# Units of one image instead of a pair, with one GroupNorm chain for both norms and one order of operations for every step

## What is computed

```python
# _gn: GroupNorm over 32 groups of 6 channels and all tokens of an image
x = x + hadamard(_gn(x))                       # 192 -> 192 channels, a fixed matrix
h = _gn(x)
h = gelu(layernorm(h @ W1.T + b1) * g1 + beta1)   # layernorm over the channels of a token
h = gelu(layernorm(h @ W2.T + b2) * g2 + beta2)
x = x + (h @ W3.T + b3)
```

## Time and profile before

| | |
|---|---|
| runs | 929.77 and 929.75 us, median 929.76 |
| profiled execution, first to last instruction | 927.5 us |
| busy: PE, DVE, ACT, POOL | 831.8, 799.5, 814.3, 551.2 us |
| DMA | 81.99 MB, mean 88 GB/s |
| chain that ended last | PE 48%, DVE 31%, ACT 10%, POOL 7% |

### The profile page before, as it was taken

The page is one execution under the profiler, slowest core; times in us unless marked ns, Lnnn a source line. Parts: engine busy times, 40 slices in busy tenths (PEclk is TensorE's granted clock), DMA queues, the critical chain, the costliest instruction groups (busy, mean ns, idle before and its releaser), DMA issues.

```text
span 927.5 us, 22221 instructions
## 1 busy us (share of the span) xinstructions
PE 831.8 (90%) x8353; PEld 552.3 (60%) x8353; DVE 799.5 (86%) x1416; ACT 814.3 (88%) x2400; POOL 551.2 (59%) x414
## 2 busy tenths in 40 slices
PE   0646889899999999999999999999999999889897
PEld 0114545556666666666666666666666667566663
DVE  6699898999999999999999999999998887745455
ACT  0687879689999999999999999999999998999982
POOL 0452544566666666666666666766766666577760
PEclk9987999999999999999999999999999999999999
DMA  9725022223323333233233232332111113121213
GB/s 265 234 69 145 1 70 69 74 69 104 107 69 108 103 105 98 81 103 108 70 110 101 94 117 70 98 113 84 59 40 55 50 36 104 40 69 35 70 36 102
DMA packets 52090, 81.99 MB, mean 88 GB/s; under 512 B 14608, under 2 KB 14736, under 8 KB 51856
## 3 DMA queue, kind: packets, MB, share of 16 engines
q1 hardware_dynamic: 51984, 80.58, 28.8%
HBM read 41.23 MB, written 39.32 MB: 87 GB/s over the span
## 4 chain that ended last, share of the span: by engine, by line
PE 48%; DVE 31%; ACT 10%; POOL 7%; issue 2%; SPq 1%; DMA 1%; ACTq 0%; DVEq 0%; POOLq 0%
PE tm L578 11%; DVE z L1248 6%; PE tm L573 5%; PE tp L590 5%; DVE X L1089 5%; DVE xs_lo L1080 4%; POOL ge_lo L943 4%; PE hl L487 4%; DVE bn L1106 3%; DVE x_lo L1230 3%; PE hl L418 3%; ACT z L729 3%; PE tm L567 3%; PE hl L516 2%; PE hl L492 2%; PE hl L511 2%
## 5 line engine op out<-in xcount | busy, mean ns | idle before, releaser
L943 POOL TENSOR_TENSOR ge_lo<-ge,ge_hi 128x512 f16<-128x512 f32 (+1 forms) x190 | 314.1, 1664 | 189.7 <-ACT ge_hi L759 189.7
L729 ACT ACTIVATE z<-tm 128x194 f32<-128x194 f32 x784 | 250.8, 346 | 41.9 <-PE tm L578 38.6
L935 POOL TENSOR_TENSOR rs<-ssq,neg_half 128x4 f32<-128x4 f32 x196 | 204.9, 1046 | 124.1 <-ACT z L729 123.2
L1248 DVE TENSOR_TENSOR z<-tm,rs 128x768 f32<-128x768 f32 x196 | 186.0, 949 | 62.1 <-POOL rs L935 61.3
L729 ACT ACTIVATION_READ_ACCUMULATOR z<-tm 128x1 f32 x784 | 175.1, 223 | 0.0
L741 ACT ACTIVATE ge<-tp,par 128x512 f32<-128x512 f32 x196 | 155.2, 792 | 21.1 <-PE tp L590 20.5
L759 ACT ACTIVATE ge_hi<-ge 128x512 f16<-128x512 f32 (+1 forms) x190 | 161.8, 855 | 2.9
L1089 DVE SCALAR_TENSOR_TENSOR X<-hl,h_bias,X 128x512 f32<-128x512 f32 x138 | 102.0, 741 | 30.6 <-PE hl L423 30.1
L590 PE MATMUL tp<-cst,z 128*128 128x128 f32 x784 | 121.8, 278 | 4.9 <-DVE z L1248 2.8
L1230 DVE SCALAR_TENSOR_TENSOR x_lo<-X,gscale,x_hi 128x512 f16<-128x512 f32 x144 | 102.8, 743 | 1.1 <-ACT x_hi L706 1.1
L590 PEld LDWEIGHTS tp<-cst,z 128*128 128x128 f32 x784 | 85.7, 142 | 28.4 <-issue 21.7
(11 more groups left out here) (192 smaller groups left out, 1888.2 us busy)
## 6 DMA issues: line engine op xcount, KB each, us to landing
out<-X SPq DMA_DIRECT2D x48, 512.0 KB, 2.9
X<-x SPq DMA_DIRECT2D x40, 512.0 KB, 4.0
out<-X SPq DMA_DIRECT2D x98, 128.0 KB, 3.0
X<-x SPq DMA_DIRECT2D x80, 128.0 KB, 4.1
X<-x SPq DMA_DIRECT2D x8, 576.0 KB, 4.2
X<-x SPq DMA_DIRECT2D x16, 144.0 KB, 4.4
X<-weights SPq DMA_DIRECT2D x1, 1024.0 KB, 12.1
out<-X SPq DMA_DIRECT2D x8, 64.0 KB, 3.0
```

The lines of the kernel that those rows point to most:

```text
L729: last = nc.scalar.activation(z[n][:, 2 * h + k, i * TW:(i + 1) * TW], tm[h][:, i, k * TW:(k + 1) * TW], ACT.Square, scale=float(C) ** -0. ...
L935: nc.gpsimd.tensor_tensor(rs[n][:, 2 * h:2 * h + 2, :], ssq[n][:, 2 * h:2 * h + 2, :], neg_half[0:TT, 0:4].rearrange("p (i k) -> p i k", i=2),
L943: nc.gpsimd.tensor_tensor(ge_lo[n][:, g % 2, PART[h], :], ge[n][:, PART[h], :], ge_hi[n][:, g % 2, PART[h], :], ALU.subtract).then_inc(s_g ...
L1248: nc.vector.tensor_tensor(z[n][:, 2 * h:2 * h + 2, 0:2 * C].rearrange("p k (i o) -> p i k o", i=2), tm[h][:, :, 0:2 * TW].rearrange("p i ( ...
```

## The change

A unit is now 512 tokens of each half of *one* image (`SIDE` = 1536 tokens a side): blocks 0 and 1 are the upper channels of the two halves, block 2 the lower channels of both. So blocks 0 and 1 share scale and bias, and `residual`, `scaled_hi`, `scaled_lo`, `split_x1` and `x1_split_lo` take them in one instruction of 1024 columns. An image has U = 3 units, X is a ring of 14 units, and the 64 leftover tokens of an image have tiles of their own (`XL`, `left`) and operations of their own at every image. A chain now comes at every third step, g = 2 mod 3, sixteen in the loop with the one at g = 0, and handles gn1 of image q + 2 and gn2 of image q in one piece; in it `w1_shift` and `h_shift` stand directly one after the other on TensorE. H runs four units ahead instead of seven, the start-up does four H units and three small chains, `first` is gone, and every step up to g = 43 uses `step`. DPOS is 46.

The diff, cut:

```diff
-PAIRS = B // 2
-U = 6
-N = U * PAIRS
+U = 3
+N = U * B
...
-H_AHEAD = U + 1
-FIRST_H = {1: (6, -1), 2: (7, 8), 3: (9, -1), 4: (10, 11)}
...
-PERIOD_STATS = (4, 4, 3, 3, 2, 2)
...
+H_AHEAD = 4
+AHEAD_STATS = 24
+FIRST_STATS = (3, 5, 4)
+PERIOD_STATS = (4, 3, 2)
...
+def chain_at(g):
...
     if g == 0:
-        return 1
...
+        return 3
+    q, r = divmod(g + 1, U)
+    return 3 + q if r == 0 and 1 <= q < B else None
...
             def scaled_hi(a, b):
...
-                nc.scalar.activation(xs_at(xs_hi, a, wide(a))[:, b, :], xcols(a, b, wide(a)), ACT.Copy,
-                                     scale=scale1(a // U, b)).then_inc(s_xs_hi, 1)
+                    nc.scalar.activation(xs_hi[:, a % 2, 0:2, :], X[:, a % RX, 0:2, :], ACT.Copy, scale=scale1(q, 0)
+                                         ).then_inc(s_xs_hi, 1)
...
             def residual(a, b):
...
+                    nc.vector.scalar_tensor_tensor(out=X[:, a % RX, 0:2, :], in0=hl[:, :, 0:UT], scalar=bias[:, 0:1],
+                                                   in1=X[:, a % RX, 0:2, :], op0=ALU.add, op1=ALU.add).then_inc(s_res, 1)
...
+            def gn_stats(j):
...
+                images = [(n, q) for n, q in enumerate(chain_images(j)) if q is not None]
+                ns = slice(images[0][0], images[-1][0] + 1)
+                for n, q in images:
+                    dve.wait_ge(s_bn[n], U * (q + 1))
+                    if j != 1:
+                        nc.vector.bn_aggr(gst[:, 0, :, n], bn[n][:, q % 2, 0:2 * U + 1, :].rearrange("p u s -> p (u s)"))
+                    for i in range(2):
+                        rows = slice(64 * i, 64 * i + 64)
+                        last = nc.vector.bn_aggr(gst[rows, 1, :, n], bn[n][rows, q % 2, 2 * U + 1:3 * U + 1 + (i == side(q)[0]), :]
+                                                 .rearrange("p u s -> p (u s)"))
...
             def step(g):
...
-                gn_stats(gn2_pair(g), 1)
-                gn_stats(gn1_pair(g), 0)
-                residual(h_unit(g, 0), 0)
+                gn_stats(chain_at(g))
+                residual(h_unit(g), 0)
                 normalise(g, 0, 0)
-                residual(h_unit(g, 0), 1)
-                stats_x1(h_unit(g, 0), 0)
-                residual(h_unit(g, 0), 2)
-                gn_var(gn2_pair(g), 1)
+                stats_x1(h_unit(g), 0)
+                residual(h_unit(g), 2)
+                gn_var(chain_at(g))
                 split_left_lo(g)
```

More of the change, by code:

```diff
@@ L442, in h_c @@
                 last.then_inc(s_h, 1)
[L443 removed]
+                held[name] = s_res, 2 * a + 2
             def h_left(a):
[L447 removed]
+                q, u = divmod(a, U)
+                if not 0 <= a < N or u < U - 1:
                     return
[L449 to L454 removed]
@@ L463, in h_left @@
-                for r, part in enumerate(parts):
-                    for i in range(2):
-                        cols = slice(64 * i, 64 * i + 64)
-                        last = nc.tensor.matmul(hl[cols, 0, REM:2 * REM], h16[:, AC_, cols], part[:, i, :], start=False,
-                                                stop=(r == 1), skip_group_check=True)
+                pe.wait_ge(s_xsl_lo, q + 1)
+                free("a")
+                i = side(q)[0]
+                parts = xsl_hi[:, i], xsl_lo[:, i]
@@ L668, in _ @@
             pe.wait_ge(s_cload, 32)
-            pe.wait_ge(s_fill, 1)
-            gn_means(0, 0)
+            gn_means(0)
             pe.wait_ge(s_h16, 1)
             h_shift(0)
-            for a in range(U):
-                h_ab(a)
-                h_c(a)
-            h_left(U - 1)
-            gn_means(0, 1)
+            h_ab(0)
+            h_c(0)
+            h_ab(1)
+            h_c(1)
+            gn_means(1)
+            h_ab(2)
+            h_c(2)
+            h_left(2)
+            h_shift(1)
+            gn_means(2)
             pe.wait_ge(s_wcen, 1)
-            w1_shift(0)
+            w1_shift(2)
+            h_ab(3)
+            h_c(3)
             pe.wait_ge(s_wlo, 3)
             pe.wait_ge(s_ones, 1)
-            run(first, step, last, drain)
+            run(step, last, drain)
         @block.scalar
@@ L1411, in _ @@
-            residual_left(U - 1)
-            for b in range(3):
-                stats_x1(U - 1, b)
-            gn_stats(0, 1)
-            stats_x(range(18, 24))
-            gn_var(0, 1)
-            stats_x(range(24, 30))
-            gn_shift(0, 1)
-            stats_x(range(30, 36))
-            gn_w1_bias(0)
-            for b in range(3):
-                x1_split_lo(0, b)
-            run(first, step, last, drain)
-def run(first, step, last, drain):
+            gn1_shift(0)
+            scaled_lo(0, 0)
@@ new lines, in _ @@
+            gn1_shift(1)
+            residual(2, 0)
+            residual(2, 2)
+            residual_left(2)
+            gn_h_bias(1)
+            stats_x1(2, 0)
+            stats_x1(2, 1)
+            stats_x1(2, 2)
+            gn_stats(2)
+            scaled_lo(3, 0)
+            gn_var(2)
+            scaled_lo(3, 2)
+            gn2_shift(2)
+            x1_split_lo(0, 0)
+            gn_w1_bias(2)
+            x1_split_lo(0, 2)
+            residual(3, 0)
+            residual(3, 2)
+            scaled_lo(h_unit(0), 0)
```

965 lines of the change are left out of this document (422 added, 543 removed).

## The result

The changed kernel takes 1006.29 us (median of 1005.53 and 1007.05) against 929.76: ratio 1.083, 95% interval 1.080 to 1.086. The forecast was 938 with a range of 915 to 953, so it is 68 us too low and the range misses by 53.

What follows compares the result with a forecast made beforehand. A step costs the larger of TensorE's and VectorE's list, with chains on the path. 927.5 + 24.0 (steady) + 6.8 (steps 36 to 47) - 15.2 (steps 0 to 5) - 7.3 (start-up) = 935.8, so 938 us as median, range 915 to 953.

Steps and rivals of the forecast that it cites:

- Start-up: Before the first z: its first chain needs three units instead of six, so z at 73.3 against 80.6, -7.3 us.
- TensorE waits for the read of the bias row: Chain step: h_shift idles some 1.1 us for VectorE's read; this alternation costs 1.4, making the step 19.5.
- the chain step's VectorE list: Chain step: VectorE alone would take 18.1 us, with gn1_shift adding 0.6.
- The clock: Steady part: a TensorE clock below full was listed as a sign the forecast is wrong, with no size.
- The plain step at 15.9: Step without chain or gn_stats: TensorE's list is unchanged, so it stays at 15.9 us.
- rival 3: Merged ScalarE part delays GpSimd; sign: second z waits over 0.8 us; 951 to 964 us, chance 15%.
- merging pays nothing here: Plain step: VectorE's merges save 0.36 us, but TensorE's matmuls hide it.
- The step that ends in `gn_stats`: A third of the steps: VectorE's list sums to 17.5 us, with TensorE's list inside it.
- The merge's price of 0.12: One merged 1024-column operation takes 1.20 us instead of 2 x 0.66, saving 0.12.
- Rival 2: The chain's wait is hidden and its operations cheap: VectorE's steps cost 17.0 and 18.1, total 911 to 924; 25%.

Runs made afterwards that it cites:

- e3: The changed kernel (1006.3 us) with h_shift and gn_h_bias of a chain moved to the same places one step later: 993.8 us.
- e2: The changed kernel with ScalarE's scaled_hi of blocks 0 and 1 moved behind gelu_hi(g - 2, 1, 1) in every step: 999.7 us.
- e8: e3 with gn1_shift alone moved to the end of its step: 960.5 us.
- e10: e8 with scaled_hi behind gelu_hi(g - 2, 1, 1) and split_left_lo behind the statistics and scaled_lo: 949.0 us.
- e11: e10 with the low parts of blocks 0 and 1 in two instructions of 512 columns: 960.4 us.
- probe: A kernel computing nothing of the reference: 24 phases, each running four equal VectorE instructions beside three equal GpSimd ones; no total time given.
- e12: e10 with gn1_shift moved to the next step, behind scaled_left_lo: 947.9 us.
- e5: e3 with gn1_shift at the end of its step and gn_w1_bias's cast and bias rows behind normalise(g - 1, 1, 1): 1017.1 us.

## Why the prediction was wrong, point by point

- **Start-up**: right within 1 us (74.3 for 73.3).
- **TensorE waits for the read of the bias row**: it does, 0.94 a time for the 1.1 forecast. But the forecast let this alternation set the chain step (19.5 over VectorE's own 18.1), and VectorE's list set it. Without the wait a step at full clock was 0.18 shorter (e3); most of e3's 12.5 us is clock.
- **The failed step is the chain step's VectorE list**, "VectorE alone would be there at 12.65 + 2.4 (four bn_stats) + 3.0 (rest of the chain) = 18.1" and "`gn1_shift` added (+0.6)". Durations were taken from the trace of before as if they were properties of the instruction. They were those of instructions that met no `gelu_lo`. At their new time `gn1_shift` lasts 1.5 instead of 0.6 and the cast 1.80 instead of 0.26, in 13 steps; 18.1 and these 2.4 make 20.5, where 20.74 was measured at the full clock. The argument also followed only one reader of what VectorE delivers (`h_shift`). It missed that `gn1_shift` stands ahead of `final_ab`, for which `w1_shift` waits (21.5 us in all), and that the next step's first group waits for the bias rows. The forecast put +0.6 into VectorE's list and kept TensorE's arrival at `w1_shift` as it was. Moving that one piece took 33.3 us off.
- **The clock** was named as a sign of error and not priced. Behind waits of 1.6 and 0.9 us, 8 of the 12 chain steps from 5 to 38 ran partly at 1.2 GHz: up to 21.9 instead of 20.7, some 9 us together, and so did step 2 (23.1).
- **The plain step at 15.9**: wrong by 0.9 to 1.4 in the changed kernel, right within 0.2 (16.1; 16.35 late) once chain steps weren't late. Its sign for rival 3 did appear: the second z waited 0.90 us for GpSimd. Rival 3 had half of the mechanism: it counted how late the power starts, and the power itself then lasted 2.0 for 1.0 beside the merged low part. That "merging pays nothing here" left this cost out. e2 and e8 both remove it, so ScalarE's order alone isn't the cause.
- **The step that ends in `gn_stats`**: `gn_stats` was 2.3 long as summed, though its aggregations have 42 numbers at 0.345 us, not the 78 that the text gave. The list without waits is 17.75 (e10), 0.25 more than summed. The other 0.65 is the wait for `left_hi` (0.35) and a `left_lo` of 64 columns that lasts 0.57 for 0.27, until GpSimd's subtraction ends: its split was priced at its duration only. e10 took both away with a move of 2 us.
- **The upper half**: not priced. Late steps that end in `gn_stats` are 0.6 to 0.7 longer and late plain ones 0.2, from image 8 on.
- **The merge's price of 0.12**: right for the instruction. The probe's low parts start 0.664 apart with 512 columns and 1.196 with 1024, so merging a pair saves 0.13; e11 lost 0.2 to 0.3 a step for two unmerged pairs. The fixed part of about 75 ns that the Trainium skill gives ("Vector Engine (DVE) Microarchitecture Reference", 5.2) is less than this, and the measurement decides.

e10 (949.0) takes 52.8 us per image early on, where 52.9 was summed, and 53.7 later. That is partly luck: its chain step no longer has the wait that made up 1.4 of the forecast's 19.5, and has instead a cast held for 0.9. Less that hold it is 18.1, which is what the forecast summed for VectorE alone. Of the 11 us between 938 and 949 some 5 are those of the late images, 3 lie in steps 0 to 5 (106.9 for 103.7, all in step 0) and 1 in the start-up. So the durations without neighbours were about right; what was missing is when the pieces meet. Rival 2's chain step, with the wait hidden, came in the end (17.7 from e12 on), but only with a new order.

## What to carry to other kernels

A duration read from a trace holds for the neighbours it had. Before an instruction of VectorE with two SBUF inputs, or a cast, is moved or added, look up what GpSimd runs at that time, and count a hold of up to that instruction's length; do the same for GpSimd's instructions when a VectorE instruction gets wider. A small piece that goes into a chain must be followed to every engine that waits for anything behind it, not only to its own reader. What is not urgent (a shift, a leftover) belongs where its engine waits anyway: four instructions of 0.6 us together were worth 33 us.

## What the runs showed of the hardware

- A cast of 192 columns takes 0.25 us alone and 1.2 beside a GpSimd subtraction of 512 columns (probe), 1.8 beside one of 1024 (L1141). An operation of 1024 columns with one input in PSUM (1.27) and bn_stats (0.68) keep their length.
- GpSimd's power of 4 columns doesn't lengthen VectorE's SBUF pairs, though it is itself longer beside them: 3.34 for three against 2.96 beside one PSUM input in the probe, and 2.0 for one of 1.0 in the changed kernel's plain steps.
- On VectorE and ScalarE, an instruction on partitions 64 to 127 next to one on all 128 gives up about 0.1 us of overlap; one on 0 to 63 doesn't.
- Equal waits of TensorE (1.62 and 0.94) were followed by the half clock in 8 chain steps of 12 and not in the other 4; waits of 3.25 (e5) in 12 steps of 13. What decides between them stays open.
